# Two-layer graph kernel: one mended row per run behind the history in place of choosing products for six of seven groups

## The reference, cut to what matters

```
h = relu(layernorm(x))
m = relu(h @ W_pool.T + b_pool)[src] * weight          # 50000 x 256
neigh = segment_max(m, dst)                            # 0 where a node has no edge
x = x + h @ W_self.T + b_self + neigh @ W_neigh.T + b_neigh
```

## Time and profile before

| | us |
|---|---|
| median of 3 runs | 1336.85 |
| lowest and highest run | 1335.12, 1338.69 |
| the profiled execution: span from first to last instruction | 1333.1 |
| the profiled execution: time of its own | none is given beside the span; the median of the runs is 3.75 above it |
| PE busy in the span | 946.2 (71%) |
| DVE busy | 927.7 (70%) |
| POOL busy | 867.5 (65%) |
| ACT busy | 615.5 (46%) |

### The profile page before, as it was taken

How to read it: one execution, slowest core, us unless ns; L and a number is a source line. 1 busy time by engine, 2 the same in 40 slices (tenths; PEclk the granted TensorE clock), 3 DMA queues, 4 the chain that set the end, 5 groups by cost and what they waited for, 6 DMA issues and landing times. The chain is left out here.

```text
span 1333.1 us, 18946 instructions
## 1 busy us (share of the span) xinstructions
PE 946.2 (71%) x5112; PEld 734.5 (55%) x5112; DVE 927.7 (70%) x2671; ACT 615.5 (46%) x1494; POOL 867.5 (65%) x884
## 2 busy tenths in 40 slices
PE   7405455555123511189997999999999999999984
PEld 6402233333012510177775777777777777777773
DVE  6466475666466554346756888888888888888758
ACT  6334333433333433323324666665656566666554
POOL 0377777777777777665237777777777777777112
PEclk9755555555555555599998999999999999999988
DMA  5667667557676665534657778778777877777322
GB/s 154 135 206 261 208 213 206 198 201 234 211 278 213 210 199 197 206 87 121 159 155 226 229 231 235 231 232 237 232 231 231 239 234 228 233 234 230 94 68 83
DMA packets 105353, 266.84 MB, mean 200 GB/s; under 512 B 25101, under 2 KB 45940, under 8 KB 99108
## 3 DMA queue, kind: packets, MB, share of 16 engines
q0 software_dynamic: 54560, 166.61, 42.7%
q1 hardware_dynamic: 48900, 97.26, 22.8%
q10 hardware_dynamic: 1792, 1.75, 0.5%
HBM read 195.59 MB, written 68.81 MB: 198 GB/s over the span
## 5 line engine op out<-in xcount | busy, mean ns | idle before, releaser
L683 POOL DMA_INDIRECT gath<-hp_d,chain_src x391 | 386.3, 988 | 169.3 <-issue 157.7
L1354 POOL DMA_INDIRECT gbuf<-pm_d,srcs x357 | 343.8, 963 | 114.7 <-issue 104.9
L924 DVE SCALAR_TENSOR_TENSOR hist<-hist,smask,gath 128x256 f32<-128x256 f32 x390 | 189.2, 485 | 207.4 <-ACT gath L716 199.6
L716 ACT ACTIVATE gath<-gath,chain_w 128x256 f32<-128x256 f32 x391 | 167.4, 496 | 335.3 <-DMA gath<-hp_d,chain_src 335.2
L1724 DVE TENSOR_TENSOR acc<-ps,acc 112x272 f32 x425 | 186.8, 440 | 70.2 <-DVE acc L1724 62.9
L1477 PE MATMUL ps<-qw,halves 128*128 x1275 | 209.9, 274 | 8.1 <-DVE halves L1709 8.1
L1479 PE MATMUL ps<-gbuf,ident 128*128 128x256 f32 x714 | 214.2, 382 | 0.0
L1565 ACT ACTIVATE gbuf<-ps 128x512 f32<-128x512 f32 x180 | 107.4, 597 | 163.8 <-PE ps L1479 163.8
L1501 PE MATMUL ps<-gbuf,placed 128*112 128x272 f32 x714 | 179.6, 393 | 0.9 <-issue 0.6
L839 PE MATMUL ps<-win_hot,node_hot 128*112 128x28 bf16 x391 | 43.6, 253 | 187.6 <-DVE win_hot L1023 187.6
L1477 PEld LDWEIGHTS ps<-qw,halves 128*128 128x128 bf16 x1275 | 125.0, 98 | 80.0 <-issue 11.2
(11 more groups left out here) (290 smaller groups left out, 1429.5 us busy)
## 6 DMA issues: line engine op xcount, KB each, us to landing
hist_d<-hist SPq DMA_DIRECT2D x48, 1024.0 KB, 4.5
gath<-hp_d,chain_src POOLq DMA_INDIRECT x391, 2.8
wn<-node_row_d SPq DMA_DIRECT2D x27, 224.0 KB
key<-node_row_d SPq DMA_DIRECT2D x26, 224.0 KB, 3.6
gbuf<-pm_d,srcs POOLq DMA_INDIRECT x357, 4.0
pm_d<-gbuf SPq DMA_DIRECT2D x6, 896.0 KB, 5.0
hb_d<-gbuf SPq DMA_DIRECT2D x7, 448.0 KB, 3.5
qw<-hb_d SPq DMA_DIRECT2D x7, 448.0 KB, 8.0
```

The lines of the kernel that those rows point to most:

```text
L683: eng.indirect_dma_start(row_at(j), None, hp_d[:, :], bass.IndirectOffsetOnAxis(ap=chain_src[:, j:j + 1], axis=0)).then_inc(got[q % RINGG] ...
L716: eng.activation(row_at(j), row_at(j), ACT.Copy, scale=chain_w[:, j:j + 1]).then_inc(gw_ready, 1)
L924: eng.scalar_tensor_tensor(out=state_at(j), in0=state_at(j - 1) if j else first_state[:, :], scalar=smask[:, j:j + 1], in1=row_at(j), op0= ...
L1354: eng.indirect_dma_start(gath3(g % RING)[:, k, 0:2 * D], None, pm_d[:, :], bass.IndirectOffsetOnAxis(ap=srcs[:, g * SG + k:g * SG + k + 1] ...
```

## The change

`hist_d` gets 128 rows more. For each run p, the row `P * CH + 1 + p` holds a mended row: the state at the end of the run's first node, maximum with the run's carry. The row number of that state is worked out as `first_end` beside the chain. POOL gathers the 128 states right after `node_rows(0)`; DVE takes the maximum with `carry` in one instruction behind `merge(0)`; SP writes the result to `hist_d`; and `end_i` of each tied node in windows 4 to 27 points to the mended row instead of the state. So `choose` and `merge` remain for group 0 alone, and `tied` is made for 4 windows instead of 28. POOL's `node_rows(1)` now waits for the write of the mended rows (`mend_out`), and what stands behind it in POOL's order waits too. `keep_warm(8)` behind the second `choose` becomes `keep_warm(16)`. `messages(i)` is no longer split. POOL makes one more small `iota` at the start of the chain, and DVE has nine small instructions more beside the chain: five in `tie` and four in `ends`.

```diff
-    hist_d = nc.dram_tensor("hist_d", [P * CH + 1, D], fp32, kind="Internal").ap()
+    hist_d = nc.dram_tensor("hist_d", [P * CH + 1 + P, D], fp32, kind="Internal").ap()
...
+        mend = up[:, 3072:3072 + D]
...
+                        eng.iota(run_i[:, :], [[0, 1]], base=1, channel_multiplier=1).then_inc(io_set2, 1)
...
                 node_rows(eng, 0, first_rows(0))
+                eng.indirect_dma_start(mend, None, hist_d[0:P * CH + 1, :],
+                                       bass.IndirectOffsetOnAxis(ap=first_end[:, 0:1], axis=0)).then_inc(mend_in, 16)
...
                 def tie():
                     first = slice(0, 1)
                     eng.tensor_scalar(tied_b[:, :], iof[:, 0:WIN], low[:, first], None, ALU.is_equal)
+                    eng.wait_ge(io_set2, 3)
+                    eng.tensor_copy(edge[:, 11:12], run_i[:, :])
+                    eng.tensor_scalar(off[:, :], own[:, :], own[:, first], 0.0, ALU.is_equal, ALU.add, accum_out=edge[:, 12:13])
                     after(eng.tensor_scalar(tied_w[:, :], iof[:, 0:NT], edge[:, 9:10], edge[:, 8:9], ALU.is_equal, ALU.mult))
+                    eng.tensor_scalar(tied_n[:, :], tied_w[:, :], edge[:, 11:12], None, ALU.mult)
+                    after(eng.scalar_tensor_tensor(out=edge[:, 13:14], in0=edge[:, 11:12], scalar=float(CH), in1=edge[:, 12:13],
+                                                   op0=ALU.mult, op1=ALU.add))
+                    eng.tensor_scalar(first_end[:, :], edge[:, 13:14], float(-(CH + 1)), None, ALU.add)
...
+                        late = slice(GN, NT)
+                        after(eng.scalar_tensor_tensor(out=end_t[:, late], in0=bank(3)[0:WIN, late], scalar=float(P * CH),
+                                                       in1=end_f[:, late], op0=ALU.add, op1=ALU.subtract))
+                        after(eng.tensor_tensor(end_t[:, late], end_t[:, late], end_0[:, late], ALU.mult))
+                        after(eng.tensor_tensor(end_f[:, late], end_f[:, late], end_t[:, late], ALU.add))
...
-                    t = at(j, J_LAST, 1, NT)
+                    t = at(j, J_LAST, 1, GN)
...
             def _(eng):
+                eng.wait_ge(mended, 1)
+                eng.dma_start(hist_d[P * CH + 1:P * CH + 1 + P, :], mend).then_inc(mend_out, 16)
                 eng.wait_ge(ngot[1], 16 * GN)
...
-                node_rows(eng, 1, first_rows(1))
                 eng.memset(power[:, :], -0.5).then_inc(power_set, 1)
                 eng.wait_ge(power_set, 1)
+                eng.wait_ge(mend_out, 16)
+                node_rows(eng, 1, first_rows(1))
...
                 def turn_n(i):
-                    eng.wait_ge(merged, i + 1)
-                    if i >= 1:
+                    if i == 0:
+                        eng.wait_ge(merged, 1)
+                    else:
+                        eng.wait_ge(ngot[i % 4], (i // 4 + 1) * (16 * GN))
                         eng.wait_ge(n_put, i)
...
                 def neigh(i):
                     eng.wait_ge(n_put, i + 1)
+                    if i >= 1:
+                        eng.wait_ge(x1_ready, i)
...
-                choose(0)
+                choose()
                 keep_warm(12)
                 turn_n(0)
                 neigh(0)
-                choose(1)
-                keep_warm(8)
+                keep_warm(16)
...
-                    messages(i, range(3))
-                    if i + 2 < NG:
-                        choose(i + 2)
-                    messages(i, range(3, GN))
+                    messages(i, range(GN))
...
+                def mend_rows():
+                    eng.wait_ge(mend_in, 16)
+                    eng.tensor_tensor(mend, mend, carry, ALU.max).then_inc(mended, 1)
...
-                merge(0)
+                merge()
+                mend_rows()
                 rows_x(0)
                 shifts(0)
-                merge(1)
...
                     if i + 1 < NG:
                         shifts(i + 1)
-                    if i + 2 < NG:
-                        merge(i + 2)
                     take(i, 3)
```

More of the change, by code:

```diff
@@ L405, in gnn_two_layers @@
         carry = acc[:, after_nt:after_nt + D]
-        keep = acc[0:WIN, after_nt + D:after_nt + D + NT]
+        keep = acc[0:WIN, after_nt + D:after_nt + D + GN]
         end_i = acc[0:WIN, after_nt + D + NT:after_nt + D + 2 * NT].bitcast(i32)
@@ L419, in node_rows @@
                 t = i * GN + k
-                eng.indirect_dma_start(to[:, k * D:(k + 1) * D], None, hist_d[:, :],
+                eng.indirect_dma_start(to[:, k * D:(k + 1) * D], None, hist_d[:, :] if i else hist_d[0:P * CH + 1, :],
                                        bass.IndirectOffsetOnAxis(ap=end_i[:, t:t + 1], axis=0)).then_inc(ngot[i % 4], 16)
@@ L457, in gnn_two_layers @@
             end_0 = s("end_0", [WIN, NT], fp32)
+            zeros_n = s("zeros_n", [WIN, NT], fp32)
             tied_b = s("tied_b", [P, WIN], fp32)
             tied_w = s("tied_w", [P, NT], fp32)
-            tied = up[:, 2560:2560 + NT * WIN]
+            tied_n = s("tied_n", [P, NT], fp32)
+            run_i = s("run_i", [P, 1], i32)
+            first_end = s("first_end", [P, 1], i32)
+            tied = up[:, 2560:2560 + GN * WIN]
             link = s("link", [P, P], fp32)
@@ L501, in gnn_two_layers @@
             ngot = [sem2(f"ngot{r}") for r in range(4)]
+            mend_in = sem2("mend_in")
             prep = sem2("prep")
@@ L871, in _ @@
                 eng.matmul(bank(1)[0:WIN, 0:NT], ones[0:WIN, 0:WIN], cnt_n[:, :], start=True, stop=True)
-                ins = eng.matmul(bank(3)[0:WIN, 0:NT], tied_b[:, :], tied_w[:, :], start=True, stop=True)
+                ins = eng.matmul(bank(3)[0:WIN, 0:NT], tied_b[:, :], tied_n[:, :], start=True, stop=True)
                 ins.then_inc(ends_in, 1)
@@ L932, in set_pads @@
                     eng.memset(zero[:, :], 0.0)
-                    eng.memset(end_0[:, :], 0.0)
+                    eng.memset(zeros_n[:, :], 0.0)
                     eng.tensor_scalar(padb[:, 0:BLK], iof[0:1, 0:BLK], 97.0, None, ALU.mult)
@@ L978, in slots @@
                     if part == 0:
-                        eng.wait_ge(io_set2, 2)
+                        eng.wait_ge(io_set2, 3)
                         eng.tensor_copy(jf[:, :], j_i[:, :])
@@ L1075, in ends @@
                         eng.wait_ge(ends_in, 1)
-                        eng.tensor_scalar(keep, bank(3)[0:WIN, 0:NT], -1.0, NEG, ALU.add, ALU.mult)
+                        tie_n = bank(3)[0:WIN, 0:NT]
+                        after(eng.tensor_scalar(end_0[:, :], tie_n, 0.0, None, ALU.is_gt))
+                        eng.tensor_scalar(keep, end_0[:, 0:GN], -1.0, NEG, ALU.add, ALU.mult)
                         after(eng.tensor_copy(end_t[:, :], bank(1)[0:WIN, 0:NT]))
-                        after(eng.tensor_tensor_scan(end_f[:, :], end_t[:, :], end_0[:, :], 0.0, ALU.add, ALU.add))
+                        after(eng.tensor_tensor_scan(end_f[:, :], end_t[:, :], zeros_n[:, :], 0.0, ALU.add, ALU.add))
                         after(eng.tensor_tensor(end_f[:, :], end_f[:, :], end_t[:, :], ALU.subtract))
@@ L1134, in _ @@
                                            ALU.add, ALU.max).then_inc(ran, 1)
-                eng.wait_ge(tied_ready, NT)
+                eng.wait_ge(tied_ready, GN)
             for old in first_sems:
@@ L1178, in gnn_two_layers @@
             chosen = sem("chosen")
+            mended = sem("mended")
+            mend_out = sem("mend_out")
             merged = sem("merged")
@@ L1359, in _, with choose @@
             def _(eng):
-                def choose(i):
-                    if i >= 1:
-                        eng.wait_ge(x1_ready, i)
+                def choose():
                     for k in range(GN):
-                        t = i * GN + k
+                        t = k
                         ins = eng.matmul(bank(0, 2)[0:WIN, k * D:(k + 1) * D], tied[:, t * WIN:(t + 1) * WIN], carry, start=True, stop=True)
@@ L1592, in _, with merge @@
                 eng.memset(onec, 1.0).then_inc(one_set, 1)
-                def merge(i):
-                    eng.wait_ge(ngot[i % 4], (i // 4 + 1) * (16 * GN))
-                    eng.wait_ge(chosen, i + 1)
+                def merge():
+                    eng.wait_ge(ngot[0], 16 * GN)
+                    eng.wait_ge(chosen, 1)
                     for k in range(GN):
-                        t = i * GN + k
-                        nk = node_rows_of(i)[:, k * D:(k + 1) * D]
+                        nk = node_rows_of(0)[:, k * D:(k + 1) * D]
                         ins = eng.scalar_tensor_tensor(out=nk, in0=bank(0, 2)[0:WIN, k * D:(k + 1) * D],
-                                                       scalar=keep[:, t:t + 1], in1=nk, op0=ALU.add, op1=ALU.max)
+                                                       scalar=keep[:, k:k + 1], in1=nk, op0=ALU.add, op1=ALU.max)
                     ins.then_inc(merged, 1)
+                def mend_rows():
```

(2 more changed lines are left out.)

1 line of the change is left out of this document (added).

## The result

The changed kernel takes 1332.88 us (median of 13 runs, 1330.06 to 1335.82), the kernel before 1336.39 us beside it on the same chip (13 runs). The ratio is 0.9976 with a 95% interval of 0.9966 to 0.9985: 3.2 us less, where the prediction had 2.85 less. The profiled executions differ by 2.0 us (span 1331.1 against 1333.1).

The account below looks back on a forecast made before the run. POOL's gather issue bounds the chain stage, a handover ring the node stage, PE the edge stage. +0.1 +1.65 +0.9 -5.3 -0.2 = -2.85 us from 1336.85 gives 1334.0 us; own range 1332.3 to 1335.5, 8-in-10 range 1330.5 to 1337.5.

Parts of the forecast that it names:

- Beside the chain: Chain stage: 6.5 us of removed DVE work gains nothing, nine small DVE instructions are covered, the `iota` adds 0.1 us.
- The seam's links: Between chain and iterations: state gather, maximum, write and POOL's wait start `node_rows(1)` at 575.1, root at 584.7; `neigh(2)` 1.65 late.
- The clock at the seam: PE idles 5.6 us ahead of `turn_h(0)`, the clock halves for 3.7 us, and `neigh(2)` comes 0.9 us later.
- rival A: Everything as forecast, but the clock stays up at the seam: -3.75 us, 1333.1 us; chance 0.20.
- From the first root to the second: Node stage: POOL has the same 12.67 us of work between the roots, so `root(1)` starts at 597.4.
- The sum of the seam: Delay at `neigh(2)`: +0.1 from the chain, +1.65 from the seam and +0.9 from the clock, 2.65 us.
- The iterations: Node stage: without `choose` and `merge`, iterations 1 to 3 save 1.77 us each, 5.3 in all; iteration 4 saves 0.2.
- Rival C: Iterations don't shorten, as ACT or a gather takes over: up to 1339.5 us, 1336.8 with half saved; chance 0.13.
- B: Seam free at `neigh(2)`, iterations give 2.2 us each, or DVE's missing instructions free POOL: 1327 to 1330 us; chance 0.10.
- The edge stage: Edge stage, PE busy 540.89 of 541.80 us: left alone by the change, as long as now.
- Rival D: Mended rows come late, each us beyond 575.1 reaching the end at full price; no gain at 3 us more; chance 0.06.

Follow-up runs that it names:

- the last run: Changed kernel with the state gather and its maximum first and 12 idle products behind `turn_n(1)`, run a second time: 1329.01 us, ratio 0.9952.
- the two partial runs: Changed kernel with four unread choosing products put back: 1532.20 us, ratio 0.9960; changed kernel with four merge-like DVE instructions put back: 1530.33 us, ratio 0.9937.

## Why the prediction was right

The sign, the mechanism and nearly the size hold; that the size comes so near is in part luck, as two errors stand against each other. By its own steps:

- **Beside the chain**: the removed DVE work taken at nothing is right (no change per gather, and the run with the work put back). The chain ended 0.27 us later, not 0.1. The gather behind the `iota` came 0.07 us later than before (1.46 for 1.39 us behind its predecessor). The rest is what two executions differ by: from the first gather to the last it is 504.27 us before, 504.55 after, and 503.64 in the last run, whose chain work is the changed kernel's.
- **The seam's links**: the state gather at 569.50 (predicted 569.21), the maximum 0.41 us (0.49), the write with POOL's wait 573.85 to 576.33, 2.48 us (2.27), `rows_h(0)` 1.30 us behind the root (1.28). The copy of the event at the chain's end was a good price. The root was 1.2 us later than forecast.
- **A clock the prediction didn't look at**: the choosing products at 568.14 ran at half rate, so the merge started at 571.86 instead of 570.62. With the fourth gather issued at 568.27 and landing in 2.64 us it could have started at 570.91; 0.95 us are the clock's and the rest is the later chain. With the longer write it makes the 1.2 us by which `node_rows(1)` and the root are later than forecast. The counts speak against the change as its cause: of the 14 traces six have these products at 3.15 to 3.61 us and eight at 1.95. One of the six is the kernel with no seam at all, and one of the eight is the changed kernel itself, run again.
- **The clock at the seam**: it fell, as forecast, and rival A is out. But the reason given doesn't hold. The forecast had a gap of 5.6 us, a little longer than the 5.0 us after which the clock had fallen ahead of the edge stage. The gap was 4.65 us, shorter than that, and the clock fell 3.4 to 4.4 us behind PE's last product; in two experiments it fell with gaps of 1.94 and 2.47 us, and with the 1.21 us of the kernel before it stayed. That the forecast of a fall came true is partly luck. Its length was mis-sized too: PE worked at the lower clock from 589.30 until between 595 and 596, about 6 us, not 3.7. It cost 0.83 us at `turn_h` and 2.16 at `neigh(1)`, 2.99 where 1.85 was forecast. POOL then stood 2.30 us at the second root waiting for the statistics: at `neigh(2)` the fall cost about 2.3 us, not 0.9.
- **From the first root to the second**: here the forecast misread a row. It took the 12.67 us of the kernel before as POOL's work. They hold an idle time of 1.73 us, which in that trace is
```profile
584.22 1.03 POOL L1337 DMA_INDIRECT qw<-blocks_d,want  x1 [1.73 <-issue]
```
It stands ahead of the first gather of edge records. The traces of the kernel before and of the kernel without the seam have it, 1.73 us in both, and none of the other twelve has more than 0.30 there; what it waits for is not shown. In the changed kernel POOL is ready for the second root after 600.12 - 2.30 - 585.88 = 11.94 us. Behind the second root the forecast has 4.96 us to `neigh(2)`, and it is 5.28.
- **The sum of the seam**: 4.65 us at `neigh(2)` against 2.65 forecast. The 2.0 us are +1.2 (POOL late from the choosing products on), +1.4 (the clock at the seam), -0.7 (POOL's stretch between the roots) and +0.1 of small terms.
- **The iterations**: 15.90, 15.95 and 15.95 us where 16.1 was forecast. That is 5.85 us saved against 5.3, and iteration 4 gave 0.36 against 0.2. The put stands right behind `q_middle`, as read from the earlier trace rows, and came 0.1 us sooner behind the start of `rows_h` than forecast (3.41 for 3.52). Rival C is out, and so is B's 2.2 for each iteration. That PE's issue is a bound just behind it is shown by the two partial runs: 1.62 for the products alone, 0.01 for the merge alone.
- **The edge stage**: 541.31 for 541.80. The prediction took it at no change. From its first product to the end of the span it is 619.85 us before, 619.41 after and 620.29 in the last run, so the half microsecond lies inside what one execution can tell.
- **The errors partly cancel**: 2.0 us too little at the seam and 0.7 too little in the iterations. The forecast of the profiled span would have been 1330.2; it was 1331.1, and the median lies the other way, 0.35 us better than forecast. The two differ because the profiled execution of the kernel before was a fast one. Time less span is 1.8 to 2.1 us in every run of the last experiment, so a span of 1333.1 belongs to a time of 1334.9 to 1335.2, 1.2 to 1.5 below the median of 1336.39, while the changed kernel's profiled execution is its median. The forecast of 1334.0 stands on the median of three runs, 1336.85, and lies 1.1 above the measured 1332.88, inside its range.
- **Two slips**: the chance of being faster by more than 0.3% adds up, by the terms given, to 0.10 + 0.10 + 0.05 = 0.25, not 0.28. And the `take` of 0.69 us ahead of the put is DVE's row; ACT's takes 0.57.

Rival D's mechanism holds as far as the first root: `node_rows(1)` came 1.2 us later than forecast and so did the root. Its amount (3 us and more) didn't occur. The other way it doesn't hold at full price: in the last run `node_rows(1)` came 4.92 us sooner and the root 2.37, for then the statistics set it. For one thing the prediction had no sight: the order on POOL could have been turned round at next to no cost, since the rows to be mended don't depend on group 0 (`neigh(0)` starts at 576.39 in the last run and at 576.20 in the changed kernel).

## What to carry to other kernels

When work moves out of a loop to a seam ahead of it, price the seam by the queue it stands in: here POOL stood 5.75 us for the new write, with eight gathers and a root behind it, and a falling clock added to that; `neigh(2)` came 4.65 us late. Issuing the new transfer four gathers sooner, with idle products over the gap, took 5.3 us back, about 1.7 of it by the idle products (an estimate, from 18.28 and 16.60 us in two experiments). Before an interval of a trace is carried over as work, take the idle times out of it: 1.73 of POOL's 12.67 us were idle time that the changed kernel doesn't have. When work goes from an engine that is nearly full, name what the next instruction in the ring waits for besides before counting the saving; here ACT's row order, on an engine busy 5.92 of 15.95 us, gave 1.77 us where 1.93 came. And an instruction that waits for another may be free by itself: the merge cost time only behind its products.

## What was not expected of the hardware

- The granted clock at the same place of nearly the same program is not fixed. In the 3.30 us that end where the choosing products start PE was busy 1.28 us in the kernel before, in the changed one and in the last run alike; it stayed at 1.00 in the first and the last and fell to 0.50 in the changed one.
- Once PE worked again at the seam the clock took about 6 us to come back. At the start of the edge stage it was 3.7 us in the kernel before, and between 2.3 and 4.6 us in the changed one and in the last run.
- A short gap was enough for a fall: with PE idle for 2.47 us, and in another kernel for 1.94, the clock went to 0.50 within 1.7 us of PE's new start, and `neigh(1)` took 5.37 us instead of 3.7 in both.
- On some chips engines stood in waits that no instruction explains, of up to 16.39 us (an ACT put), and the same kernel took 1521 to 1541 us instead of 1336. POOL's gathers were as long there as elsewhere (983 to 991 ns).
- A DVE instruction can hold up POOL's gathers after all, though those of 0.27 us beside the chain didn't. In the node stage DVE adds two SBUF tiles of 112x1024 in 1.22 us (L1668; L1638 in the kernel before). A gather that starts while this runs ends 2.0 us after the addition's start wherever it began: one that starts 0.13 us into it takes 1.90 us (592.23, the addition at 592.10), one that starts 0.91 into it 1.12 us (589.86 and 588.95 in the last run), where most take 0.93. It is so in all 14 traces. That it is held until the addition ends fits these times; no run varies the addition.
